# A four-layer graph kernel on one core: raw row-block loads issued as four transfers of 32 partitions from two queues

## The chip, the cores and the metric

The kernel runs on one core of a Trainium2 chip. The metric is the device time of one execution in microseconds (us), the median of the timed runs. All data are 32-bit floats.

## What is computed

Four graph layers act in turn on x (5120 nodes, 64 features) with one dense adjacency matrix adj (5120 x 5120, 105 MB). Each layer normalises x over its features, applies relu, multiplies by adj in its own way and adds the result to x:

```python
h = relu(layernorm(x)); x = x + L0(h, adj, ...)   # e = h + small product; adj @ (adj.T @ e), normalised, + h
h = relu(layernorm(x)); x = x + adj @ h           # L1
h = relu(layernorm(x)); x = x + L2(h, adj, ...)   # three products with adj, one after another
h = relu(layernorm(x)); x = x + L3(h, adj, ...)   # adj with unit diagonal, scaled by its row sums (degrees)
```

## The kernel before

The program has two stages. In the first, adj is read once from the chip's memory, is turned (transposed) on the way and is written back turned, as `adj_t`; at the same time the two products of the first layer and the row sums are made. In the second, five passes stream tiles of `adj_t` back in for the products that are left.

**Stage one.** adj is cut into 7 groups of columns (g), six of 768 columns and a last one of 512, and into 10 row blocks of 512 rows (m). A raw load brings one row block of one group, 128 partitions by 4 by 768 (1.5 MB), into `raw[:, m]`. Two row blocks make a pair, and five pairs make a group. A period of the steady state handles one pair, and the engines do this in it:

- TensorE turns the pair `after` into four PSUM banks that are used in rotation (`turn_banks`, L654), multiplies the pair before it, already turned, by t (`product_for_h`, L719 and L630), and multiplies two raw row blocks of the next group by E (`products_for_t`, L635 and L641). `products_for_t` waits for the raw load (L637).
- ScalarE copies each turned bank to `staged` (`copy_banks`, L853 and L869); TensorE needs the copy before it reuses the bank.
- VectorE turns the last chunk of each pair itself (`turn_chunk`, L1088 and L1105) and sums rows of raw (`sum_rows`, L1013 and L1016). Both wait for the raw load.
- The sync engine, SP, issues all large transfers in one order, written out by hand (L587 to L596): load of the first block of a pair for the next group, store of the turned pair (3 MB, L560), load of the second block. `load_next` (L567) waits until TensorE and VectorE have turned the pair (`wait_turned`) and until its rows are summed, since the load overwrites the same space.

Each raw load increments `raw_in[m]` by 16, and whoever reads waits for `g * 16 + 16`.

At the start SP issues the loads of x (three parts) and ten first loads (`load_first`, L545). ScalarE issues six small loads (L876 to L881), then copies `diag`, then squares and copies in turn for each row block (L882 to L890): these squares feed the first normalisation, and the chain ScalarE, VectorE, GpSimd, VectorE, TensorE is repeated per block until `e_ready` has reached 10. Then group 0 begins (L952).

**Stage two** begins near 523 us. Its tile loads (`load_turned`, L574) are issued by SP alone and span 128 partitions.

Of the kernel before, what the change touches and what calls it, by code (L numbers as in the profile page):

```python
# [10 lines left out]
P = 128  # L11
# [31 lines left out]
OPEN_BANKS = 5  # L43
EPS = 1e-5
SQ = 32
STAGE_WORDS = CHUNKS * PAIR
TILE_WORDS = 2 * PAIR

# [187 lines left out]
def gnn_stack(nc, x_d, adj_d, wu_d, du_d, pu_d, wi_d, di_d, pi_d, gam_d, bet_d, w2_d, b2_d, w3_d, b3_d, out_d):  # L236
    plan = Plan()
    ctx = ExitStack()
    with ctx:
# [188 lines left out]
        def raw_of(g, m):  # L428

            return raw_last[:, m] if g == NG - 1 else raw[:, m]  # L430
# [28 lines left out]
        def banks(g, m):  # L459

            return range(2 * chunks(g) - 2 * by_vector(g, m))
# [77 lines left out]
        @block.sync  # L539
        def _(sp):  # L540
            def load_x(i):
                t = slice(X_PARTS[i][0] * SUB, X_PARTS[i][1] * SUB)
                sp.dma_start(X[:, t, :], x_v[:, t, :]).then_inc(x_in[i], 16)

            def load_first(m):  # L545
                sp.dma_start(raw[:, m], adj_v[:, m, :, 0:GW]).then_inc(raw_in[m], 16)

            load_x(0)
            sp.dma_start(diag_rows[0:U // P, :], du_d.rearrange("(t p) -> t p", p=P)).then_inc(diag_in, 16)
            sp.dma_start(diag_rows[U // P:NT, :], di_d.rearrange("(t p) -> t p", p=P)).then_inc(diag_in, 16)  # L550
            load_x(1)
            load_first(0)
            load_x(2)
            for m in range(1, NB):
                load_first(m)

            def store(g, m):
                wait_copied(sp, g, m)
                at = g * CHUNKS * PAIR
                sp.dma_start(adj_t[m, :, at:at + STAGE_WORDS], staged_pair(g, m)).then_inc(stored_by(g, 2 * m)[0], 16)  # L560

            def store_kept(u):
                wait_copied(sp, NG - 1, u // 2, u % 2)
                at = (NG - 1) * CHUNKS * PAIR + u % 2 * TILE_WORDS
                sp.dma_start(adj_t[u // 2, :, at:at + TILE_WORDS], turned_into(NG - 1, u)).then_inc(stored_by(NG - 1, u)[0], 16)

            def load_next(g, m):  # L567

                wait_turned(sp, g, m // 2)
                sp.wait_ge(deg_summed, SUM_NO[g, m])  # L570
                src = adj_v[:, m, :, (g + 1) * GW:(g + 1) * GW + chunks(g + 1) * P]
                sp.dma_start(raw_of(g + 1, m), src).then_inc(raw_in[m], 16)

            def load_turned(n):  # L574

                p, m, k, dual = plan.tiles[n]
                j = plan.slot[n]
                sp.dma_start(whole[j], adj_t[m, :, k * TILE_WORDS:(k + 1) * TILE_WORDS]).then_inc(whole_in[j], 16)

            def first_load(n):  # L580
                p, m, k, dual = plan.tiles[n]
                g = (2 * k + 1) // CHUNKS
                for u in (2 * m, 2 * m + 1):
                    sp.wait_ge(*stored_by(g, u))
                load_turned(n)

            store(0, 0)  # L587
            load_next(0, 0)
            load_next(0, 1)
            for g in range(NG - 1):  # L590
                for i in range(ROWS):
                    after = (g, i + 1) if i + 1 < ROWS else (g + 1, 0)
                    if after[0] < NG - 1:
                        load_next(after[0], 2 * after[1])
                        store(*after)
                        load_next(after[0], 2 * after[1] + 1)  # L596
            first = iter(plan.loads[:len(AT_START)])
            first_load(next(first))
            sp.wait_ge(*stored_by(NG - 2, UNITS - 3))
            sp.wait_ge(used, unit_no(NG - 2, UNITS - 2))  # L600
            for _ in range(STAGE_WORDS // TILE_WORDS):
                first_load(next(first))
            store_kept(0)
            store_kept(1)
            sp.wait_ge(*stored_by(NG - 2, UNITS - 1))
            sp.wait_ge(used, unit_no(NG - 1, 0))
            for _ in range(LATE_SLOTS + 1 - STAGE_WORDS // TILE_WORDS):
                first_load(next(first))
            for u in range(2, UNITS):
                if u == UNITS - 1:  # L610
                    wait_turned(sp, NG - 1, u // 2)
                    sp.wait_ge(deg_summed, SUM_NO[NG - 1, u])
                    for n in first:
                        first_load(n)
                store_kept(u)
            for u in range(UNITS - 2, UNITS):
                sp.wait_ge(*stored_by(NG - 1, u))
            sp.wait_ge(used, TOTAL_UNITS)
            for n in plan.loads[len(AT_START):]:
                sp.wait_ge(multiplied, plan.used_no(plan.slot_before[n]))  # L620
                load_turned(n)
# [3 lines left out]
        def _(pe):  # L625
# [8 lines left out]

            def products_for_t(g, m):  # L635

                pe.wait_ge(raw_in[m], g * 16 + 16)  # L637
                columns = chunks(g) * P // 2
                for a in range(SUB):
                    for h in range(2):  # L640
                        last = nc.tensor.matmul(t_acc[h * D:(h + 1) * D, 0:columns], E[:, m * SUB + a, :],  # L641
                                                raw_of(g, m)[:, a, h * columns:(h + 1) * columns],
                                                start=(m == 0 and a == 0), stop=(m == NB - 1 and a == SUB - 1))
                if m == NB - 1:
                    last.then_inc(t_done, 1)
# [192 lines left out]
        def _(act):  # L838
# [33 lines left out]
            def copy_unit(g, u, some):  # L872

                copy_banks(g, u // 2, [u % 2 * chunks(g) + i for i in some if u % 2 * chunks(g) + i in banks(g, u // 2)])

            for i, src in ((0, pu_d), (2, pi_d)):  # L876
                act.dma_start(par[:, i:i + 2], src.partition_broadcast(P)).then_inc(early_in, 16)
            act.wait_ge(made, 2)
            for i, src in ((0, wu_d), (1, wi_d)):
                for h in range(2):  # L880
                    act.dma_start(w_in[h * D:(h + 1) * D, i, h * D:(h + 1) * D], src).then_inc(early_in, 16)  # L881
            act.wait_ge(diag_turned, 1)  # L882
            nc.scalar.activation(diag[:, :], t_rows[:, 0:NT], ACT.Copy).then_inc(diag_ready, 1)
            for m in range(NB + 2):
# [44 lines left out]
            def group(g):  # L929
                for i in range(ROWS):  # L930
                    after = (g, i + 1) if i + 1 < ROWS else (g + 1, 0)
                    begun = BEGUN if (g, i) == (0, 0) else 0
                    if i == 0:
                        copy_t(g)
                    copy_banks(*after, range(begun, TURN_BANKS))
                    if i == 0:
                        take_t(g)
                    copy_banks(*after, banks(*after)[TURN_BANKS:])

            def last_group():  # L940
                g = NG - 1
# [8 lines left out]
                    end_of_layer(u)  # L950

            act.wait_ge(e_ready, NB)  # L952
            for g in range(NG - 1):
                group(g)
            last_group()
# [37 lines left out]
        def _(dve):  # L993
# [18 lines left out]

            def sum_rows(g, m):  # L1013

                dve.wait_ge(raw_in[m], g * 16 + 16)
                nc.vector.tensor_reduce(deg_part[:, of(m), g], raw_of(g, m), AX.X, ALU.add).then_inc(deg_summed, 1)  # L1016


# [69 lines left out]
            def turn_chunk(g, m):  # L1088

                if by_vector(g, m):  # L1090
                    for b in range(2):
                        dve.wait_ge(raw_in[2 * m + b], g * 16 + 16)
                    if g < NG - 1:
                        wait_stage_free(dve, g, m)
                    elif m >= 1:
                        wait_turned(dve, g, m - 1)
                    else:
                        wait_turned(dve, g - 1, ROWS - 1)
                    half, c = chunks(g) // 2, chunks(g) - 1
                    rows = raw_flat if g < NG - 1 else raw_flat[:, 0:NB * SUB * CHUNKS_LAST * P]  # L1100
                    src = rows[:, :].rearrange("p (m a h k) -> p m h a k", m=ROWS, h=2, k=chunks(g) * P)[:, m]
                    dst = turned_into(g, 2 * m + 1)[:, (half - 1) * PAIR:half * PAIR].rearrange("p (h a n) -> p h a n", h=2, a=SUB)
                    for q in range(4):
                        for b in range(4):
                            last = nc.vector.transpose(dst[b * SQ:(b + 1) * SQ, :, :, q * SQ:(q + 1) * SQ],  # L1105
                                                       src[q * SQ:(q + 1) * SQ, :, :, c * P + b * SQ:c * P + (b + 1) * SQ])
                    last.then_inc(vector_turned, 1)
# [189 lines left out]
```

## Time and profile before

| what | value |
|---|---|
| timed runs | 1457.35 and 1459.07 us, median 1458.21 us |
| profiled execution, first to last instruction (span) | 1456.2 us |
| mean granted TensorE clock over the span | 0.997 |
| TensorE busy | 1422.6 us (98%) |
| moved by DMA | 523.23 MB, mean 359 GB/s |

The profiled execution's own time is its span and what lies around it. The page gives the span alone; the median of the timed runs is 2.0 us above it, and that is taken as what lies around. A busy share of TensorE counts modelled ends of pipelined matmuls, so a full share does not by itself say that TensorE is the bound: the timeline has to show that it never waits.

### The profile page before, as it was taken

To read this page: it belongs to the slowest core of one execution; us is meant where nothing else is said; L and a number is where in the kernel's file an instruction comes from. 1 tells how busy PE (TensorE), PEld (TensorE's weight loads), DVE (VectorE), ACT (ScalarE), POOL (GpSimd) and SP (SyncE) were. 2 spreads that over 40 slices of the span, in tenths; PEclk is the share of its full clock that TensorE was granted. 3 is DMA by queue.
4 is the path that set the end of the run, shared out by engine and by line. 5 is a ranking of instruction groups with operands and counts; after the bars stand their busy time and mean duration, and the time that the engine had idled before them with its cause. 6 is when DMAs were issued, how large, how long until landed. Compare 5 with 4: busy or idle time off the path is not lost.

```text
span 1456.2 us, 18041 instructions
## 1 busy us (share of the span) xinstructions
PE 1422.6 (98%) x7601; PEld 601.7 (41%) x7601; DVE 665.2 (46%) x1136; ACT 226.3 (16%) x453; POOL 84.3 (6%) x67
## 2 busy tenths in 40 slices
PE   6998999999999999999999999999999999999998
PEld 3553555555555554333333333333333333333332
DVE  6699999999998734320221311011311021101044
ACT  2331423333233342000000000000000000000000
POOL 2300000000000028100000000000000000000000
PEclk9999999999999999999999999999999999999999
DMA  9998999999999998999996897989797848996998
GB/s 325 386 379 354 406 415 418 411 419 413 412 416 368 381 418 324 421 421 420 420 420 211 323 354 298 359 323 315 300 348 263 302 179 362 392 380 228 354 415 321
DMA packets 97604, 523.23 MB, mean 359 GB/s; under 512 B 18764, under 2 KB 18804, under 8 KB 54644
## 3 DMA queue, kind: packets, MB, share of 16 engines
q1 hardware_dynamic: 90436, 520.40, 91.1%
q10 hardware_dynamic: 7088, 1.67, 0.5%
q8 instruction: 61, 1.00, 0.3%
q14 instruction: 19, 0.16, 0.0%
HBM read 415.88 MB, written 106.17 MB: 359 GB/s over the span
## 4 chain that ended last, share of the span: by engine, by line
PE 61%; DMA 2%; DVE 1%; POOL 0%; issue 0%; ACT 0%; DVEq 0%
PE turned L630 33%; PE acc L630 25%; DMA over_wide<-adj_t 2%; PE turned L663 1%; PE turned L815 1%; PE t_rows L799 0%; PE turned L821 0%; DVE staged L1143 0%; PE t_acc L789 0%; PE t_acc L715 0%; PE t_rows L715 0%; POOL rstd L1246 0%; DVE staged L1001 0%; DVE X L1189 0%; DVE staged L1205 0%
## 5 line engine op out<-in xcount | busy, mean ns | idle before, releaser
L1016 DVE TENSOR_REDUCE deg_part<-raw 128x4 f32<-128x3072 f32 (+1 forms) x70 | 220.8, 3196 | 0.9
L641 PE MATMUL t_acc<-raw,E 128*64 128x384 f32 (+1 forms) x1120 | 187.2, 483 | 10.8 <-DMA raw<-in_adj_dram 10.7
L1105 DVE STREAM_TRANSPOSE staged<-raw 32x256 f32<-32x256 f32 x448 | 195.1, 436 | 5.8
L869 ACT ACTIVATE staged<-turned 128x512 f32<-128x512 f32 x303 | 152.7, 640 | 240.8 <-PE turned L663 240.4
L630 PE MATMUL acc<-staged,t_cur 128*64 128x512 f32 x720 | 161.1, 597 | 0.0
L663 PEld LDWEIGHTS turned<-ident,raw 128*128 128x128 f32 x1376 | 150.1, 141 | 25.5 <-issue 25.5
L663 PE MATMUL turned<-ident,raw 128*128 128x128 f32 x1376 | 160.5, 275 | 0.0
L630 PE MATMUL turned<-over_last,C 128*64 128x512 f32 x672 | 152.1, 592 | 0.0
L641 PEld LDWEIGHTS t_acc<-raw,E 128*64 128x64 f32 x1120 | 79.4, 139 | 115.4 <-issue 89.2
L1246 POOL TENSOR_TENSOR rstd<-rstd,minus_half 128x8 f32<-128x8 f32 (+1 forms) x30 | 44.2, 1474 | 1279.6 <-DVE rstd L1007 1279.6
L630 PE MATMUL turned<-over_last,R 128*64 128x512 f32 x512 | 116.5, 593 | 0.0
L1217 DVE TENSOR_TENSOR staged<-turned,part 128x512 f32<-128x512 f32 x11 | 7.6, 692 | 225.8 <-PE turned L630 191.7
L630 PE MATMUL acc<-over_last,R 128*64 128x512 f32 x440 | 100.0, 593 | 0.0
L1143 DVE STREAM_TRANSPOSE staged<-staged 32x128 f32<-32x128 f32 x304 | 92.0, 303 | 4.5
L630 PEld LDWEIGHTS turned<-over_last,C 128*64 128x64 f32 x672 | 48.3, 137 | 95.4 <-issue 95.4
L630 PE MATMUL acc<-over_last,C 128*64 128x512 f32 x384 | 86.6, 593 | 0.0
L630 PEld LDWEIGHTS acc<-staged,t_cur 128*64 128x64 f32 x720 | 48.9, 137 | 90.8 <-issue 90.8
L1217 DVE TENSOR_TENSOR staged<-acc,part 128x512 f32<-128x512 f32 x8 | 5.5, 690 | 151.7 <-PE acc L630 83.5
L630 PE MATMUL turned<-over_last,E 128*64 128x512 f32 x320 | 74.1, 593 | 0.0
L630 PEld LDWEIGHTS turned<-over_last,R 128*64 128x64 f32 x512 | 36.2, 137 | 71.2 <-issue 69.3
L630 PE MATMUL acc<-staged,R 128*64 128x512 f32 x264 | 60.9, 595 | 0.5 <-DMA staged<-adj_t 0.5
L630 PEld LDWEIGHTS acc<-over_last,R 128*64 128x64 f32 x440 | 31.1, 137 | 61.6 <-issue 59.0
(137 smaller groups left out, 893.6 us busy)
## 6 DMA issues: line engine op xcount, KB each, us to landing
over_last<-adj_t SPq DMA_DIRECT2D x181, 1024.0 KB, 8.9
staged<-adj_t SPq DMA_DIRECT2D x91, 1024.0 KB, 9.7
raw<-in_adj_dram SPq DMA_DIRECT2D x60, 1536.0 KB, 18.4
adj_t<-staged SPq DMA_DIRECT2D x30, 3072.0 KB, 17.1
over_wide<-adj_t SPq DMA_DIRECT2D x23, 1024.0 KB, 7.1
raw<-in_adj_dram SPq DMA_DIRECT2D x10, 1024.0 KB, 15.0
adj_t<-over_last SPq DMA_DIRECT2D x8, 1024.0 KB, 12.2
adj_t<-C SPq DMA_DIRECT2D x2, 1024.0 KB, 21.7
```

What stands on the lines that cost most here:

```text
L630: last = nc.tensor.matmul(bank[h * D:(h + 1) * D, :], v[:, t + c, :], tile[:, (2 * c + h) * B:(2 * c + h + 1) * B], start=start and c == 0 ...
L641: last = nc.tensor.matmul(t_acc[h * D:(h + 1) * D, 0:columns], E[:, m * SUB + a, :], raw_of(g, m)[:, a, h * columns:(h + 1) * columns], st ...
L663: last = nc.tensor.transpose(turned[n % TURN_BANKS][:, a * P:(a + 1) * P], raw_of(g, 2 * m + b)[:, sub, c * P:(c + 1) * P], ident[:, :])
L815: last = nc.tensor.matmul(weigh_bank[odd][:, i * 4 * D:(i + 1) * 4 * D], feat_t[rows, nodes], w0123[rows, :, :].rearrange("p w d -> p (w d ...
L869: nc.scalar.activation(turned_into(g, u)[:, i * B:(i + 1) * B], turned[n % TURN_BANKS][:, :], ACT.Copy) \
L1016: nc.vector.tensor_reduce(deg_part[:, of(m), g], raw_of(g, m), AX.X, ALU.add).then_inc(deg_summed, 1)
L1105: last = nc.vector.transpose(dst[b * SQ:(b + 1) * SQ, :, :, q * SQ:(q + 1) * SQ], src[q * SQ:(q + 1) * SQ, :, :, c * P + b * SQ:c * P + (b ...
L1143: last = nc.vector.transpose(dst[b * SQ:(b + 1) * SQ, :, h, e, :], src[q * SQ:(q + 1) * SQ, :, b, :])
L1217: ins = nc.vector.tensor_tensor(y_sb[r % 2], bank, part[:, m, :], ALU.add)
L1246: op.tensor_tensor(v, v, minus_half[:, t(0)], ALU.pow).then_inc(pow_ready, 1)
```

## The change

Each raw load becomes four transfers of 32 partitions. SP issues those of partitions 0 to 63, ScalarE those of partitions 64 to 127. The semaphore then counts 64 for a load. ScalarE gets the ten first loads behind its six small ones, a `load_next` for blocks 0 and 1 behind its wait for `e_ready`, and one for each pair behind that pair's copies.

```diff
+QUARTERS = [slice(q * SQ, (q + 1) * SQ) for q in range(4)]
+SP_QUARTERS, ACT_QUARTERS = QUARTERS[:2], QUARTERS[2:]
+RAW_IN = 16 * len(QUARTERS)
 # SP
             def load_first(m):
-                sp.dma_start(raw[:, m], adj_v[:, m, :, 0:GW]).then_inc(raw_in[m], 16)
+                for q in SP_QUARTERS:
+                    sp.dma_start(raw[q, m], adj_v[q, m, :, 0:GW]).then_inc(raw_in[m], 16)
...
-                sp.dma_start(raw_of(g + 1, m), src).then_inc(raw_in[m], 16)
+                for q in SP_QUARTERS:
+                    sp.dma_start(raw_of(g + 1, m)[q], src[q]).then_inc(raw_in[m], 16)
 # TensorE, and the same in sum_rows and turn_chunk of VectorE
-                pe.wait_ge(raw_in[m], g * 16 + 16)
+                pe.wait_ge(raw_in[m], RAW_IN * (g + 1))
 # ScalarE
+            def load_first(m):
+                for q in ACT_QUARTERS:
+                    act.dma_start(raw[q, m], adj_v[q, m, :, 0:GW]).then_inc(raw_in[m], 16)
+            def load_next(g, m):
+                wait_turned(act, g, m // 2)
+                act.wait_ge(deg_summed, SUM_NO[g, m])
+                src = adj_v[:, m, :, (g + 1) * GW:(g + 1) * GW + chunks(g + 1) * P]
+                for q in ACT_QUARTERS:
+                    act.dma_start(raw_of(g + 1, m)[q], src[q]).then_inc(raw_in[m], 16)
...
+            for m in range(NB):
+                load_first(m)
             act.wait_ge(diag_turned, 1)
...
                     copy_banks(*after, banks(*after)[TURN_BANKS:])
+                    if after[0] < NG - 1:
+                        for m in range(2):
+                            load_next(after[0], 2 * after[1] + m)
...
             act.wait_ge(e_ready, NB)
+            for m in range(2):
+                load_next(0, m)
             for g in range(NG - 1):
```

ScalarE at the program's start, before (`par` and `w_in` are small weights, `staged<-h_acc` the squares of the first normalisation):

```order
L877 DMA par<-in_L_gnn_par_u_dram 128x2
L877 DMA par<-in_L_gnn_par_i_dram 128x2
L881 DMA w_in<-in_L_gnn_W_u_dram 64x64 [waits made]
L881 DMA w_in<-in_L_gnn_W_u_dram 64x64
L881 DMA w_in<-in_L_gnn_W_i_dram 64x64 x2
L883 ACT_TABLE_LOAD
L883 ACTIVATE diag<-t_rows 128x40 [waits diag_turned]
L845 ACTIVATE staged<-h_acc 128x256 [waits centred] x3
```

The same place of the changed program:

```order
L894 DMA par<-in_L_gnn_par_u_dram 128x2
L894 DMA par<-in_L_gnn_par_i_dram 128x2
L898 DMA w_in<-in_L_gnn_W_u_dram 64x64 [waits made]
L898 DMA w_in<-in_L_gnn_W_u_dram 64x64
L898 DMA w_in<-in_L_gnn_W_i_dram 64x64 x2
L883 DMA raw<-in_adj_dram 32x4x768 x20
L902 ACT_TABLE_LOAD
L902 ACTIVATE diag<-t_rows 128x40 [waits diag_turned]
L850 ACTIVATE staged<-h_acc 128x256 [waits centred] x3
```

Twenty transfers now stand ahead of ScalarE's first activation.

ScalarE from one pair of the steady state to the next, before (`staged<-turned` are the copies of a pair's ten turned banks; the waits on `used` and `stored` are for room in `staged`):

```order
L869 ACTIVATE staged<-turned 128x512 [waits used,stored0,chunk_turned]
L869 ACTIVATE staged<-turned 128x512 [waits chunk_turned] x9
L869 ACTIVATE staged<-turned 128x512 [waits used,stored1,chunk_turned]
L869 ACTIVATE staged<-turned 128x512 [waits chunk_turned] x9
L869 ACTIVATE staged<-turned 128x512 [waits used,stored0,chunk_turned]
```

The same place of the changed program:

```order
L874 ACTIVATE staged<-turned 128x512 [waits used,stored0,chunk_turned]
L874 ACTIVATE staged<-turned 128x512 [waits chunk_turned] x9
L891 DMA raw<-in_adj_dram 32x4x768 [waits deg_summed,vector_turned,chunk_turned]
L891 DMA raw<-in_adj_dram 32x4x768
L891 DMA raw<-in_adj_dram 32x4x768 [waits deg_summed,vector_turned,chunk_turned]
L891 DMA raw<-in_adj_dram 32x4x768
L874 ACTIVATE staged<-turned 128x512 [waits used,stored1,chunk_turned]
L874 ACTIVATE staged<-turned 128x512 [waits chunk_turned] x9
```

Between the copies of one pair and those of the next ScalarE now waits for VectorE's part of the pair (`vector_turned`) and issues four transfers. On SP the order of loads and stores stays, with two transfers of 32 partitions in place of each raw load.

## Rows read from the trace of the kernel before

**Rows 1.** The page, its head and its first part: busy time by engine.

```profile
span 1456.2 us, 18041 instructions
...
PE 1422.6 (98%) x7601; PEld 601.7 (41%) x7601; DVE 665.2 (46%) x1136; ACT 226.3 (16%) x453; POOL 84.3 (6%) x67
```

**Rows 2.** Stretches: length, busy by engine, then granted clock, DMA share, GB/s.

```profile
45.00:60.00 15.00, 15.00 (x96) 7.39 (x92) 7.60 (x7) 1.75 (x4) 4.63 (x1) 1.00 1.02 409
...
135.00:150.00 15.00, 10.49 (x60) 6.72 (x60) 14.77 (x20) 4.64 (x10) 0.00 (x0) 0.77 1.02 419
...
435.00:450.00 15.00, 14.84 (x95) 7.83 (x94) 13.85 (x19) 5.13 (x12) 0.00 (x0) 1.00 1.02 417
...
800.00:1000.00 200.00, 199.87 (x938) 67.17 (x936) 34.71 (x96) 5.75 (x11) 1.64 (x1) 1.00 0.87 330
```

**Rows 3.** Timeline of TensorE in steady periods: start, length, what, [idle before].

```profile
250.66 4.58 PE L663 MATMUL turned<-ident,raw 128*128 128x128 f32 x40
...
265.64 4.59 PE L663 MATMUL turned<-ident,raw 128*128 128x128 f32 x40
...
433.75 4.59 PE L663 MATMUL turned<-ident,raw 128*128 128x128 f32 x40
...
446.38 2.80 PE L641 MATMUL t_acc<-raw,E 128*64 128x384 f32 x16 [0.17 <-DMA raw<-in_adj_dram]
449.12 1.97 PE L663 MATMUL turned<-ident,raw 128*128 128x128 f32 x16
```

**Rows 4.** DMA issues: count, KB each, median us from issue to landing.

```profile
raw<-in_adj_dram SPq DMA_DIRECT2D x60, 1536.0 KB, 18.4
adj_t<-staged SPq DMA_DIRECT2D x30, 3072.0 KB, 17.1
```

**Rows 5.** Who waited for whom, whole span: total us, times, longest.

```profile
PEld t_acc L641 <- DMA raw<-in_adj_dram: 20.7, 17, 6.2
```

**Rows 6.** Issues by line: duration min/median/max in ns, first and last start.

```profile
L546 SPq DMA_DIRECT2D raw<-in_adj_dram x10: 532/3754/6989, 2.8 to 31.0; - x10
...
L987 ACTq DMA_DIRECT2D out_dram<-staged x5: 378/378/410, 1409.5 to 1453.2; - x5
```

**Rows 7.** Timeline of ScalarE at the start and at its late small loads.

```profile
3.24 1.27 ACTq L881 DMA_DIRECT2D w_in<-in_L_gnn_W_i_dram  x2
...
6.57 0.20 ACT L883 ACTIVATE diag<-t_rows 128x40 f32<-128x40 f32 x1 [0.74 <-PE t_rows L673]
...
55.17 0.45 ACTq L896 DMA_DIRECT2D b<-in_L_gnn_b_dram  x1
```

**Rows 8.** Timeline: VectorE in the first chain, SP's first next load, its first reader.

```profile
9.30 0.42 DVE L1011 SCALAR_TENSOR_TENSOR h_acc<-h_acc,rstd 128x256 f32<-128x256 f32 x1
...
11.50 0.16 DVE L1032 TENSOR_TENSOR par<-par 128x1 f32<-128x1 f32 x1 [1.78 <-DMA w_in<-in_L_gnn_W_i_dram]
...
40.61 4.31 SPq L572 DMA_DIRECT2D raw<-in_adj_dram  x2
...
70.06 5.33 PE L641 MATMUL t_acc<-raw,E 128*64 128x384 f32 x32
```

**Rows 9.** DMA queues (q10 is ScalarE's): packets, MB, share of 16 engines.

```profile
q10 hardware_dynamic: 7088, 1.67, 0.5%
```

**Rows 10.** Timelines of VectorE and ScalarE: the late VectorE, and a steady period.

```profile
105.97 5.01 ACT L869 ACTIVATE staged<-turned 128x512 f32<-128x512 f32 x10 [9.97 <-PE turned L663]
122.15 5.00 ACT L869 ACTIVATE staged<-turned 128x512 f32<-128x512 f32 x10 [11.18 <-PE turned L663]
...
112.58 7.17 DVE L1105 STREAM_TRANSPOSE staged<-raw 32x256 f32<-32x256 f32 x16
...
428.93 7.18 DVE L1105 STREAM_TRANSPOSE staged<-raw 32x256 f32<-32x256 f32 x16
...
434.44 5.00 ACT L869 ACTIVATE staged<-turned 128x512 f32<-128x512 f32 x10 [10.36 <-PE turned L663]
449.23 0.49 ACT L903 ACTIVATE t_t<-t_acc 128x384 f32<-128x384 f32 x1 [9.78 <-PE t_acc L641]
```

More of the change, by code:

```diff
@@ L1013, in sum_rows @@
             def sum_rows(g, m):
-                dve.wait_ge(raw_in[m], g * 16 + 16)
+                dve.wait_ge(raw_in[m], RAW_IN * (g + 1))
                 nc.vector.tensor_reduce(deg_part[:, of(m), g], raw_of(g, m), AX.X, ALU.add).then_inc(deg_summed, 1)
@@ L1091, in turn_chunk @@
                     for b in range(2):
-                        dve.wait_ge(raw_in[2 * m + b], g * 16 + 16)
+                        dve.wait_ge(raw_in[2 * m + b], RAW_IN * (g + 1))
                     if g < NG - 1:
```

## The prediction, on record before the changed kernel ran

> **What bounds the kernel now.** I read the page's head first, then the stretches, then TensorE's timeline, then who waits for the raw loads. The head shows a span of 1456.2 us with TensorE busy 98% of it [rows 1]; the reader is to see that TensorE is nearly always at work, and to ask whether anything else is as full. The stretches answer that: between 435 and 450 us TensorE is busy 14.84 of 15 us and the DMA engines have a share of 1.02 at 417 GB/s, so both are full at once; between 800 and 1000 us, in stage two, TensorE is busy 199.87 of 200 us at a DMA share of 0.87 [rows 2]. Stage two is TensorE's alone, and the change does not touch it. The question is stage one.
>
> There the timeline gives the two paces. A period is from the first turn of a pair to that of the next. From 250.66 to 265.64 it is 14.98 us and TensorE's rows show no wait. From 433.75 to 449.12 it is 15.37 us, and the second block of the pair is waited for, by 0.17 us beyond the last matmul [rows 3]. So late in the stage the transfers set the pace. The bytes agree: two loads of 1536 KB and a store of 3072 KB [rows 4] are 6.29 MB, and at 417 GB/s that is 15.1 us. In all, raw loads are waited for 20.7 us [rows 5]. That is the most that a better delivery of loads could give back; whatever slows the loads is paid almost one for one, since no slack is left in 14.98 against 15.1 us.
>
> **The start of ScalarE.** Twenty transfers come ahead of its first activation. Its six small loads end at 3.24 + 1.27 = 4.51 us, each of the last two having taken 0.64 us [rows 7]; its cheapest issue of the trace took 378 ns [rows 6]. At a middle 0.5 us, twenty take 10 us, and ScalarE is free at 14.5 us; before, it ran its first activation at 6.57 us, when its input was there [rows 7]. The chain behind it: VectorE's first normalised block came at 9.30 us, 2.73 us later, and ran 0.42 us; the step behind that then waited for a small load until 11.50 us [rows 8]. Now the block ends at 14.5 + 2.73 + 0.42 = 17.65 us, 17.65 - 11.50 = 6.2 us later than the step could go on. Nothing catches that up: TensorE is busy 15.00 of 15 us between 45 and 60 us [rows 2]. I take **+6.2 us**. Below: at 378 ns an issue ScalarE is free at 12.1 us, and +3.7 us is left. Above: SP's ten first issues took 3754 ns in the median and up to 6989 [rows 6], so an issue can be held until earlier ones drain; the last began at 31.0 us. Were ScalarE held until 31 us, the cost would be +22.7 us. I stay near the lower end, since ScalarE's queue has half the bytes of SP's queue of before.
>
> **The steady state on ScalarE.** Each pair adds four issues behind its copies. In the late period the copies run from 434.44 to 439.44 us and the next activation comes 9.78 us after that; four issues at 0.45 us (the last of the small late loads [rows 7]) are 1.8 us and lie in that gap. The new wait for VectorE ends before it begins: VectorE's part ran from 428.93 to 436.11 us [rows 10]. The exception is where VectorE is late: its part ran from 112.58 to 119.75 us, ScalarE's copies ended at 110.98, and the next were due at 122.15 [rows 10]. ScalarE stands there until 119.75, issues until 121.6, and the copies queued behind it are still in time, with 0.5 us to spare. If the cover fails there, TensorE, which needs the copies for its banks, pays 2 us once or twice. The first next loads move more: before at 40.61 us, now behind the late small loads, which end at 55.62 us [rows 7]; their reader starts at 70.06 us [rows 8]. That leaves 14.4 us against a median landing of 18.4 for a whole load [rows 4]. ScalarE's queue is then empty and holds half a load, so I take 0, with 4 us as the other end.
>
> **More transfers.** 70 raw loads become 280 transfers, 210 more. Each ends in small packets. ScalarE's queue of before moved only small ones: 7088 packets in 0.5% of 16 engines' span [rows 9], which is 0.005 x 1456.2 x 16 / 7088 = 16 ns each. One per engine and transfer gives 210 x 16 ns = **+3.4 us**; below, 0, as the packets may fall into idle time.
>
> **The pace of a 32-partition load.** This is the term that decides, and the trace cannot show it: every large transfer of before spans 128 partitions. The descriptors stay as they were (one row of 768 floats), so the lower bound is the present pace, 417 GB/s, and +0. The upper bound: a transfer that reaches a quarter of the partitions at a time goes at half pace. Then the 3.15 MB of loads of a period take 15.1 instead of 7.55 us, +7.5 us a period. From 145 us, where VectorE is no longer late, to the stage's end near 523 us there are (523 - 145) / 15.2 = 25 periods with DMA as full as this. So the bound is 25 x 7.5 = +188 us. Below zero: -20.7 us, all waits for raw loads gone [rows 5]; more is excluded, since TensorE's own 14.98 us remain.
>
> Between them I reason from the order. ScalarE's queue loads partitions 64 to 127, SP's 0 to 63. While both are loading, the whole width is written and the pace should hold. But SP also has the store, 3.15 MB, ahead of its second load; ScalarE has 1.57 MB in all per period, SP 4.72. If the queues share evenly, ScalarE's part runs out beside the store, and SP's 1.57 MB of loads then goes alone, on half of the partitions. All of it alone at half pace is +3.8 us a period, none is 0. I take half, +1.9 us, nearer to the row of today's pace than to the upper end: 25 x 1.9 = **+47.5 us**.
>
> The Trainium skill, SBUF — State Buffer, "Door 1: The DMA port swizzle (why `[64,N]` ≈ `[32,N]`)", speaks against the change: partitions 0 to 31 reach 8 of 16 ports, partitions 0 to 63 the same 8, and 189 GB/s were measured for 32 partitions against 328 for 128. No run here shows it. Its section "Can I just issue two DMAs to hit both halves?" adds that two concurrent transfers at partitions 0 and 64 gained only 6% over one; by that, loads stay near half pace and the sum is that of the second rival below.
>
> **The sum.** The profiled execution's span is 1456.2 us; 2.0 us more give the median of the timed runs, 1458.2. With +6.2, +3.4 and +47.5 it comes to **1515 us**.
>
> **The rivals.**
> 1. *The loads keep their pace.* The halves of the two queues overlap, and only the start and the packets cost: 1458.2 + 6.2 + 3.4 = 1468 us. For it: descriptors and bytes are the same, and the DMA share of 1.02 [rows 2] says that it is the engines that are full, whose work is unchanged. Against it: SP's queue has three times the bytes of ScalarE's. It decides if ScalarE's loads last as long as SP's loads do.
> 2. *Half pace throughout.* 1468 + 188 = 1656 us. For it: the order puts the two quarters of one queue one behind the other. Against it: two queues on opposite halves run at once. Here TensorE would wait several us in each period, and its clock may go: after the wait between 135 and 150 us, where it was busy 10.49 of 15 us, the granted clock averaged 0.77 in that stretch [rows 2], against 1.00, so some of it was granted at the lower level, 1.2 GHz.
> 3. *Faster: loads arrive earlier.* ScalarE's half of the second block is not behind the store. If that ends the waits for raw loads and the start is hidden, 1458.2 - 20.7 = 1437 us. Against it: SP's half still stands behind the store, and a load counts when its last quarter has landed. It begins to decide only if the queues together move more than 417 GB/s.
>
> That the change does not do what it says is no rival: the order shows the transfers on both engines.
>
> **How the numbers follow.** Forecast 0.44, rival one 0.40, rival two 0.12, rival three 0.04. A measurement of this kernel can tell about 2% from no change, 29 us: faster is below 1429, slower above 1487. Rival three reaches faster with its tail, 0.03. Same takes rival one but for a costly start (0.36), the rest of rival three (0.01) and the lower tail of the forecast (0.05): 0.42. Slower is what is left, 0.55. The range holds the time 8 times in 10: from 1461, just under rival one with the cheapest start (1465), to 1640, which leaves out most of rival two. The forecast's own range is 1490 to 1570. Most of the chance lies on the side of a cost; a gain over 2% has hardly any.
>
> **What would show it.** Right: ScalarE's first activation near 14.5 us; steady periods near 17 us in place of 15.37, with waits for raw loads on TensorE in each; GB/s below 417 in stage one at a DMA share that stays near 1; stage two as long as before. Wrong: periods still at 15.4 us (rival one), near 22 us (rival two), or 14.98 without waits (rival three); or a ScalarE that is held beyond 20 us at the start, which would make the start the largest term.

## The result, and the profile after

The changed kernel takes 1520.01 us (median; the runs are 1517.52 and 1522.5) against 1458.21: a ratio of 1.0423, 95% interval 1.0406 to 1.0440. It is slower by 62 us. The prediction said 1515. The sum was right, but three of its terms were not: the start was put far too low, the pace and the packets too high, and the errors nearly cancelled.

The page of the changed kernel: head, busy time, the two hardware queues (packets, MB, share of 16 engines), and the issues (count, KB each, median us to landing).

```profile
span 1515.3 us, 18310 instructions
...
PE 1426.8 (94%) x7601; PEld 602.7 (40%) x7601; DVE 665.0 (44%) x1136; ACT 226.3 (15%) x453; POOL 84.3 (6%) x67
...
q1 hardware_dynamic: 73636, 467.98, 80.7%
q10 hardware_dynamic: 27248, 54.11, 11.8%
...
raw<-in_adj_dram SPq DMA_DIRECT2D x120, 384.0 KB, 20.0
raw<-in_adj_dram ACTq DMA_DIRECT2D x120, 384.0 KB, 15.9
```

TensorE does the same work as in [rows 1], 1426.8 against 1422.6 us, in a span that is 59.1 us longer: nearly all of the lost time is idle time of TensorE. A quarter of a load (384 KB) takes 20.0 us (SP) and 15.9 us (ScalarE) to land, about as long as a whole load of 1536 KB did [rows 4].

Where it was lost is read from a landmark that occurs once per group. TensorE's `t_rows` product comes seven times, once per group; shown are the first, second, sixth and last of these marks, first before, then after.

```profile
60.94 0.49 PE L706 MATMUL t_rows<-ident,t_t 128*128 128x128 f32 x3
146.96 0.49 PE L706 MATMUL t_rows<-ident,t_t 128*128 128x128 f32 x3
...
450.92 0.49 PE L706 MATMUL t_rows<-ident,t_t 128*128 128x128 f32 x3
520.71 0.38 PE L706 MATMUL t_rows<-ident,t_t 128*128 128x128 f32 x2
```

```profile
89.64 0.55 PE L711 MATMUL t_rows<-ident,t_t 128*128 128x128 f32 x3 [1.56 <-ACT t_t L922]
178.61 0.49 PE L711 MATMUL t_rows<-ident,t_t 128*128 128x128 f32 x3
...
511.64 0.49 PE L711 MATMUL t_rows<-ident,t_t 128*128 128x128 f32 x3
580.36 0.38 PE L711 MATMUL t_rows<-ident,t_t 128*128 128x128 f32 x2
```

The difference of the pairs is 28.7, 31.7, 60.7 and 59.7 us. So 28.7 us are lost before the first mark, some 31 more through stage one, and nothing after it (span: +59.1). Of these 31, 3.0 come up to the second mark and 29.1 in the 20 periods from the second to the sixth, which take 333.0 us in place of 304.0; 1.1 are won back behind it.

**The start.** ScalarE's timeline after, and one row of VectorE's.

```profile
4.55 30.09 ACTq L883 DMA_DIRECT2D raw<-in_adj_dram  x20
...
35.97 0.20 ACT L902 ACTIVATE diag<-t_rows 128x40 f32<-128x40 f32 x1
```

```profile
38.81 0.16 DVE L1056 TENSOR_TENSOR par<-par 128x1 f32<-128x1 f32 x1
```

The twenty issues end at 34.64 us, not at 14.5. ScalarE's first activation comes at 35.97 in place of 6.57, and the step of VectorE that had gone on at 11.50 [rows 8] goes on at 38.81, 27.3 us later. Here is the spread of these issues (ns, minimum, median, maximum):

```profile
L883 ACTq DMA_DIRECT2D raw<-in_adj_dram x20: 453/644/8273, 4.6 to 26.4; - x20
```

A median of 644 ns is close to what was assumed; but single issues stand for up to 8.3 us. The engine's own work waits behind them.

The queues in the first 40 us, after and then before (the last row in each is the third part of x, us to landing):

```profile
q10 hardware_dynamic: 2506, 5.27, 63.5%
q1 hardware_dynamic: 5653, 2.57, 36.0%
...
X<-in_x_dram SPq DMA_DIRECT2D x1, 640.0 KB, 41.9
```

```profile
q1 hardware_dynamic: 9201, 13.17, 94.2%
...
X<-in_x_dram SPq DMA_DIRECT2D x1, 640.0 KB, 11.2
```

In that time ScalarE's queue (q10) brought 5.27 MB and SP's 2.57: for most of it mainly partitions 64 to 127 were being loaded, and x's third part took 30.7 us longer to land.

**The pace.** Stretches after, columns as in [rows 2], then one of before.

```profile
20.00:25.00 5.00, 0.00 (x0) 0.00 (x0) 0.00 (x0) 0.00 (x0) 0.00 (x0) 1.00 1.07 217
...
45.00:50.00 5.00, 5.00 (x22) 2.12 (x22) 3.60 (x8) 0.42 (x1) 1.11 (x1) 1.00 1.03 336
50.00:55.00 5.00, 4.67 (x34) 3.01 (x33) 4.87 (x9) 1.05 (x3) 1.11 (x1) 1.00 1.04 321
...
60.00:65.00 5.00, 5.00 (x37) 3.21 (x37) 4.90 (x8) 1.34 (x3) 0.83 (x1) 1.00 1.04 201
...
300.00:400.00 100.00, 92.54 (x587) 49.88 (x585) 86.02 (x115) 31.16 (x63) 0.00 (x0) 1.00 1.02 382
...
800.00:1000.00 200.00, 199.88 (x944) 67.74 (x942) 43.51 (x121) 8.52 (x17) 3.27 (x2) 1.00 0.83 323
```

```profile
300.00:400.00 100.00, 99.52 (x624) 52.53 (x622) 92.46 (x121) 32.58 (x66) 0.00 (x0) 1.00 1.02 414
```

The reader is to see a DMA share of 1 or more in every stretch of stage one, at rates that differ by a factor of two: 217 GB/s while ScalarE's queue loads its half and SP's is busy with x, 321 to 336 while both load, 201 when x has landed and SP's half alone is left, 382 in the steady state with the store among them, 414 before. A full share says that the engines are occupied, not that they move what they can. Stage two (800 to 1000) is as before.

A steady period on TensorE after, and its waits for raw loads over the whole span (us, times, longest):

```profile
308.36 2.80 PE L646 MATMUL t_acc<-raw,E 128*64 128x384 f32 x16 [1.34 <-DMA raw<-in_adj_dram]
311.09 4.59 PE L668 MATMUL turned<-ident,raw 128*128 128x128 f32 x40
...
324.90 2.80 PE L646 MATMUL t_acc<-raw,E 128*64 128x384 f32 x16 [1.34 <-DMA raw<-in_adj_dram]
327.63 2.62 PE L668 MATMUL turned<-ident,raw 128*128 128x128 f32 x22
```

```profile
PEld t_acc L646 <- DMA raw<-in_adj_dram: 56.1, 29, 3.6
```

This period is 327.63 - 311.09 = 16.54 us, 1.17 more than the late 15.37 of [rows 3] and 1.56 more than the earlier 14.98; the second block of each pair is waited for by 1.34 us, where it was 0.17 or nothing. The mean of the 20 periods between the marks is 29.1 / 20 = 1.45 us more than before.

Within a period the loss can be placed. The two queues between 303 and 306 us, while both load and no packet of the store is among them (packets, MB, share):

```profile
q10 hardware_dynamic: 163, 0.45, 52.3%
q1 hardware_dynamic: 164, 0.45, 51.5%
```

They move 300 GB/s together. Between 309 and 315 us, with the store among them, it is 411 to 427; before, no 1.5 us between 433 and 448 us had less than 356. ScalarE's queue does not run dry in this period: in each stretch of 3 us from 300 to 333 its share is 9.7% or more.

### The profile page after: what moved, and what is told of

The parts are those of the page before. It is cut to its first block, busy times and chain, and to the rows that moved or that the text cites. A ratio compares the mean times of both kernels' runs of the same rounds, so it can differ in the third digit from the quotient of the medians.

```text
span 1515.3 us, 18310 instructions
## 1 busy us (share of the span) xinstructions
PE 1426.8 (94%) x7601; PEld 602.7 (40%) x7601; DVE 665.0 (44%) x1136; ACT 226.3 (15%) x453; POOL 84.3 (6%) x67
## 2 busy tenths in 40 slices
DMA packets 100966, 523.26 MB, mean 345 GB/s; under 512 B 22124, under 2 KB 22164, under 8 KB 58004
## 4 chain that ended last, share of the span: by engine, by line
PE 58%; DMA 2%; DVE 1%; POOL 0%; issue 0%; ACT 0%; DVEq 0%
PE turned L635 31%; PE acc L635 24%; DMA over_wide<-adj_t 2%; PE turned L668 1%; PE turned L820 1%; PE t_rows L804 0%; PE turned L826 0%; DVE staged L1167 0%; PE t_acc L794 0%; PE t_acc L720 0%; PE t_rows L720 0%; POOL rstd L1270 0%; DVE staged L1227 0%; DVE staged L1241 0%; DVE staged L1035 0%
## 5 line engine op out<-in xcount | busy, mean ns | idle before, releaser
L646 PE MATMUL t_acc<-raw,E 128*64 128x384 f32 (+1 forms) x1120 | 191.0, 486 | 37.3 <-DMA raw<-in_adj_dram 37.3
## 6 DMA issues: line engine op xcount, KB each, us to landing
raw<-in_adj_dram ACTq DMA_DIRECT2D x120, 384.0 KB, 15.9
```

## The experiments

Unless said otherwise, each edit is made on the changed kernel, and costs in us are (ratio - 1) x 1458.2. Where the number of transfers of a load changes, the counts that readers wait for change with it; these lines are left out of the cuts.

**One part alone (two kernels).** The first loads whole again, by SP; only the next ones split:

```diff
 # load_first
-for q in SP_QUARTERS: sp.dma_start(raw[q, m], adj_v[q, m, :, 0:GW]) ...
+sp.dma_start(raw[:, m], adj_v[:, m, :, 0:GW]) ...
-ScalarE: for m in range(NB): load_first(m)
```

> The changed kernel, but the ten first loads are again one transfer of 128 partitions each, by SP; the later loads stay in quarters on two queues. Theory A (the start costs 27 us because ScalarE's issues are held until 34.67 us, the rest of the 62 us is a slower period): about 1520 - 27 = 1493 us, ScalarE's first activation at 6.6 us, steady periods still 16.5 us. Rival B (the whole loss is the pace of narrow loads in the steady state, the late start is hidden): 1515 to 1520 us.

Measured: 1489.0 us, ratio 1.0210 [1.0193, 1.0227], +30.6 us. ScalarE's first activation is at 6.75 us, and the waits in the periods stay (1.32 and 0.96 us at 311.50 and 327.99).

The reverse: only the first loads split, the next ones whole and by SP.

```diff
 # load_next
-for q in SP_QUARTERS: sp.dma_start(raw_of(g + 1, m)[q], src[q]) ...
+sp.dma_start(raw_of(g + 1, m), src) ...
-ScalarE: load_next(...)
```

> The kernel of before, but with the ten first loads in quarters on two queues as in the changed kernel; all later loads are one transfer by SP. Theory A: 1458 + 27 = 1485 us, first activation of ScalarE near 34.7 us, steady periods 15.0 to 15.4 us as before. Rival B: 1458 to 1465 us.

Measured: 1487.29 us, 1.0199 [1.0183, 1.0214], +29.0 us. ScalarE is held as in the changed kernel (its twenty issues take 30.71 us); the stretch from 300 to 400 us is back at before's rate:

```profile
300.00:400.00 100.00, 99.34 (x625) 52.62 (x623) 92.86 (x126) 30.91 (x62) 0.00 (x0) 1.00 1.02 416
```

30.6 + 29.0 = 59.6 us of 61.7: two separate costs that add up, each about half.

**Four transfers of 128 partitions.** As many transfers, the same two queues, the same rows of 768 floats; but each transfer takes one of the four rows of a partition, over all partitions.

```diff
-QUARTERS = [slice(q * SQ, (q + 1) * SQ) for q in range(4)]
+QUARTERS = [slice(q, q + 1) for q in range(4)]
-raw[q, m], adj_v[q, m, :, 0:GW]
+raw[:, m, q], adj_v[:, m, q, 0:GW]
```

> The changed kernel with the same four transfers per load, two by SP and two by ScalarE, but each takes all 128 partitions and one of the four rows of a partition, in place of 32 partitions and all four rows. Theory A (the pace is lost because a quarter, and one queue's two quarters, reach only half of the partitions): steady periods back at 15.0 to 15.4 us, DMA near 417 GB/s; the first loads drain at twice the pace, so ScalarE is free near 17 us in place of 34.67 and the start costs about 10 us: 1468 to 1472 us. Rival C (the cost is that there are four transfers and two queues): 1515 to 1520 us, periods 16.5 us.

Measured: 1479.84 us, 1.0147 [1.0132, 1.0162], +21.4 us: far from the rival's time, but above the theory's 1468 to 1472.

```profile
4.59 18.05 ACTq L883 DMA_DIRECT2D raw<-in_adj_dram  x20
```

```profile
15.00:20.00 5.00, 0.00 (x0) 0.00 (x0) 0.00 (x0) 0.00 (x0) 0.00 (x0) 1.00 1.06 375
```

At 375 GB/s in place of 217, ScalarE is still held until 22.64 us. So the hold is not made by the half width, only lengthened by it. Its first `t_rows` comes at 76.39 us, 15.5 late, and stage one ends 542.01 - 520.71 = 21.3 late: the pace costs 6 us in place of 31.

**The same width, first loads whole.**

```diff
 # on the kernel above: load_first as in the first experiment
```

> First loads whole by SP as in the kernel before; later loads as four transfers of all 128 partitions and one row each, two by SP and two by ScalarE. Theory A (the pace depends on the width alone): 1456 to 1462 us, periods 15.0 to 15.4 us. Rival G (two queues cost something of their own: the wide rows run had periods of 15.8 to 16.3 us late in the stage): 1463 to 1470 us.

Measured: 1462.48 us, 1.0032 [1.0021, 1.0042], +4.7 us. Against the first experiment (+30.6) only the shape of the next loads differs.

**The same width, all by SP.**

```diff
 # on the kernel of four wide transfers
-for q in SP_QUARTERS: sp.dma_start(...)
+for q in QUARTERS: sp.dma_start(...)
-ScalarE: load_first, load_next
```

> Every raw load as four transfers of all 128 partitions and one row each, all issued by SP, none by ScalarE. Theory A (width sets the pace; the small loss of the two-queue wide run, 1462.5 us, is the two queues' own): 1456 to 1460 us. Rival H (that small loss is the number of transfers): 1461 to 1465 us.

Measured: 1453.83 us, 0.9973 [0.9963, 0.9983], 3.9 us faster than before. The same 280 transfers cost nothing in sum. The two kernels differ by 8.6 us (4.7 + 3.9), but not in the second queue alone: one has its first loads whole, the other in four wide transfers. The first `t_rows` of the kernel on two queues, then that of this one:

```profile
60.85 0.55 PE L710 MATMUL t_rows<-ident,t_t 128*128 128x128 f32 x3 [0.38 <-ACT t_t L919]
```

```profile
58.48 0.49 PE L711 MATMUL t_rows<-ident,t_t 128*128 128x128 f32 x3
```

So 2.4 us lie before the first mark; 525.22 - 516.89 = 8.3 us lie between the two at the last. What is left for the second queue at full width is some 6 us.

**The quarters of 32 partitions, all by SP.**

```diff
-for q in SP_QUARTERS: sp.dma_start(raw[q, m], ...)
+for q in QUARTERS: sp.dma_start(raw[q, m], ...)
-ScalarE: load_first, load_next
```

> Quarters of 32 partitions as in the changed kernel, but all four issued by SP, one behind the other, none by ScalarE. Theory A (a quarter alone goes at half pace; only the other queue's quarters on the other half of the partitions bring some of it back): steady periods near 15.4 + 7.5 = 22.9 us, stage one about 190 us longer, 1640 to 1680 us; the first loads at about 210 GB/s. Rival D (what costs is the issue on ScalarE): 1460 to 1470 us.

Measured: 1626.48 us, 1.1150 [1.1074, 1.1227], +168 us, somewhat under the theory's 1640 to 1680. TensorE's timeline with its first `t_rows`, and the stretch:

```profile
92.04 0.49 PE L711 MATMUL t_rows<-ident,t_t 128*128 128x128 f32 x3
...
333.17 4.59 PE L668 MATMUL turned<-ident,raw 128*128 128x128 f32 x40
...
350.85 5.33 PE L646 MATMUL t_acc<-raw,E 128*64 128x384 f32 x16 [5.21 <-DMA raw<-in_adj_dram]
356.11 4.59 PE L668 MATMUL turned<-ident,raw 128*128 128x128 f32 x40
...
373.66 1.53 PE L668 MATMUL turned<-ident,raw 128*128 128x128 f32 x12
```

```profile
300.00:400.00 100.00, 79.92 (x457) 41.09 (x454) 71.07 (x95) 23.03 (x47) 0.00 (x0) 0.90 1.01 306
```

Here are periods of 22.9 us, the half pace of the prediction's second rival, but also of 17.6 us. The mean of the 20 between the second and the sixth mark (200.59 and 601.00 us) is 20.0, so the second rival's size is not reached; why the periods differ was not taken apart. What the changed kernel has over this one is ScalarE's queue on the other half. The granted clock from 300 to 400 us is 0.90, so part of it ran at 1.2 GHz; this follows the waits of up to 5.2 us. The first mark is 31.1 us late although ScalarE issues no raw load and runs its first activation at 6.78 us: here TensorE waits for the first raw blocks, by up to 4.98 us at a time. So first loads at half pace are costly at the start even where nothing holds ScalarE.

**Both queues on the same half at once.** SP takes quarters 0 and 2, ScalarE 1 and 3.

```diff
-SP_QUARTERS, ACT_QUARTERS = QUARTERS[:2], QUARTERS[2:]
+SP_QUARTERS, ACT_QUARTERS = QUARTERS[0::2], QUARTERS[1::2]
```

> The changed kernel, but SP takes partitions 0 to 31 and 64 to 95 of each load and ScalarE 32 to 63 and 96 to 127, so that the two queues work on the same half of the partitions at the same time. Theory A (the halves 0 to 63 and 64 to 127 each go at half pace, and only opposite halves together bring some of it back): nearly nothing is brought back, periods of 19 to 22 us, about as the kernel with all quarters on SP (1626 us) or somewhat slower, since the start is late as well: 1620 to 1660 us. Rival E (any two quarters from two queues go at the same pace, whichever they are): 1515 to 1525 us.

Measured: 1574.51 us, 1.0800 [1.0778, 1.0822], +117 us. Its second and sixth `t_rows`:

```profile
180.96 0.49 PE L711 MATMUL t_rows<-ident,t_t 128*128 128x128 f32 x3
...
562.84 0.49 PE L711 MATMUL t_rows<-ident,t_t 128*128 128x128 f32 x3
```

The 20 periods take 381.9 us, 19.1 each. Single ones reach 329.73 - 308.98 = 20.8 us, with waits of 4.4 and 4.0 us. The first mark is that of the changed kernel (89.77 and 89.64 us), so the difference lies in the pace. The bytes, transfers and queues are those of the changed kernel; which partitions the queues reach at the same time makes 55 us. The time lies between the two that were expected. That the queues do not stay in step would make the loss smaller than the theory's; this is not shown.

**Halves of 64 partitions.** One transfer for each queue, the same two halves.

```diff
-QUARTERS = [slice(q * SQ, (q + 1) * SQ) for q in range(4)]
-SP_QUARTERS, ACT_QUARTERS = QUARTERS[:2], QUARTERS[2:]
+QUARTERS = [slice(q * 2 * SQ, (q + 1) * 2 * SQ) for q in range(2)]
+SP_QUARTERS, ACT_QUARTERS = QUARTERS[:1], QUARTERS[1:]
```

> The changed kernel with two transfers per load, SP partitions 0 to 63 and ScalarE 64 to 127, in place of four: half the number of transfers, the same halves and queues. Theory A (what counts is the half that a queue reaches, not the number of transfers): 1512 to 1522 us, periods 16.5 us, ScalarE held to about 30 us at the start. Rival C (the number of transfers costs): half of the loss is gone, about 1490 us.

Measured: 1522.38 us, 1.0439 [1.0423, 1.0454]: the changed kernel's time with half its transfers. Its first `t_rows`:

```profile
90.71 0.49 PE L711 MATMUL t_rows<-ident,t_t 128*128 128x128 f32 x3
```

ScalarE's ten issues of 768 KB end at 29.39 us, 5.3 us earlier than the changed kernel's twenty, and yet the first mark is 1.1 us later. So the hold alone does not set the mark; x's third part took 43.3 us to land here.

**Fewer first loads on ScalarE.** Only the first five blocks are split at the start; SP loads the other five whole.

```diff
 # load_first, SP
+if m < 5: quarters as now
+else: sp.dma_start(raw[:, m], ...)
-ScalarE: for m in range(NB): load_first(m)
+ScalarE: for m in range(5): load_first(m)
```

> The changed kernel, but only the first five row blocks come in quarters at the start, ten transfers by ScalarE in place of twenty; the other five come whole from SP. Theory A (ScalarE is held because its queue is full: 34.67 us was reached when about 86 of its 160 row packets per engine had gone, so some 75 fit): ten transfers are 80 packets and nearly fit, ScalarE is free at 10 to 13 us, and the start costs 2 to 10 us in place of 28: 1495 to 1503 us. Rival F (each issue on ScalarE takes 1.5 us beside a busy SP): free at 4.6 + 15 = 20 us, the start costs 14 us, about 1506 us.

Measured: 1512.53 us, 1.0370 [1.0339, 1.0402]. ScalarE's ten issues end at 10.27 us, as the theory had it; but little was won, since something else was late next:

```profile
38.02 0.69 PE L690 MATMUL t_rows<-ident,staged 128*128 128x128 f32 x2 [12.04 <-DVE staged L1064]
...
80.90 0.55 PE L714 MATMUL t_rows<-ident,t_t 128*128 128x128 f32 x3 [2.67 <-ACT t_t L925]
```

VectorE had waited for the third part of x, which took 31.4 us to land. It stands behind the first raw load in SP's queue. The first mark is still 20.0 us late, and the time is above both that were expected.

**The same, with x's third part ahead of the first raw load on SP.**

```diff
 load_x(1)
+load_x(2)
 load_first(0)
-load_x(2)
```

> As the run with ten first transfers on ScalarE (1512.5 us), and SP issues the third part of x ahead of its first raw load. Theory A (there TensorE stood 12 us at 38 us because the third part of x, 160 small packets per engine, went one for one with ScalarE's slow row packets and landed at 35.8 us): the part lands before 12 us, that wait is gone and the start costs 2 to 8 us: 1492 to 1498 us. Rival I (what is late at the start is the raw blocks, since they come at half pace): 1508 to 1513 us.

Measured: 1509.08 us, 1.0336 [1.0305, 1.0368]: the theory missed, and the time is the rival's. x lands in 15.0 us, the wait of 12 us is gone, and the first `t_rows` comes at 69.41:

```profile
69.41 0.55 PE L714 MATMUL t_rows<-ident,t_t 128*128 128x128 f32 x3 [1.19 <-ACT t_t L925]
```

So up to this mark the start now costs 8.5 us. But TensorE waits for the first next loads instead, 6.12 us at 84.87 and 5.49 at 95.36, and of the 20.2 us won against the changed kernel at the first mark 8.9 are left at the last. So not all of what the start costs can be had by mending it alone; how the rest is lost was not taken apart further.

**The store behind both loads.** An edit on the kernel before: SP's order for a pair becomes load, load, store.

```diff
 load_next(after[0], 2 * after[1])
-store(*after)
 load_next(after[0], 2 * after[1] + 1)
+store(*after)
```

> The kernel of before with one change in SP's order: both whole loads of a pair are issued ahead of the store, in place of load, store, load. If the waits for raw loads that are left (20.7 us) come from the second load standing behind the 3 MB store, most of them go and the time is 1440 to 1450 us. If the DMA engines' own work per period sets the pace (15.1 to 15.3 us against 14.98 us of TensorE), the store comes late in place of the load: 1453 to 1460 us.

Measured: 1450.21 us, 0.9947 [0.9935, 0.9960]: 7.7 us faster than before, and so faster than both kernels. Its `t_rows`, and its waits (us, times, longest) on transfers:

```profile
136.15 0.49 PE L706 MATMUL t_rows<-ident,t_t 128*128 128x128 f32 x3
...
510.10 0.38 PE L706 MATMUL t_rows<-ident,t_t 128*128 128x128 f32 x2
```

```profile
ACT staged L869 <- DMA adj_t<-staged: 53.7, 8, 10.2
```

It is 10.8 us ahead of before at the second mark, 6.6 at the third (215.58 against 222.18 us) and 10.6 at the last; its span is 8.2 us shorter. So the early waits, which are also where before's clock fell to 0.77 [rows 2], are the largest part of the gain; some of it is given back at once, and the last group wins again. TensorE's waits for raw loads are gone from the view. In their place ScalarE now waits for room in `staged`; where TensorE feels that, it is 2.27 us at 138.91.

**Both gains together.** The store last, on the four wide transfers by SP.

```diff
 # the kernel with all wide transfers on SP
 load_next(after[0], 2 * after[1])
-store(*after)
 load_next(after[0], 2 * after[1] + 1)
+store(*after)
```

> The four transfers of 128 partitions by SP alone, with the store behind both loads of a pair. Theory (their two gains have different places, the first chain at the start and the waits for raw loads in the steady state, and add up): 1458.2 - 4.4 - 8.0 = 1445.8 us, 1444 to 1448. Rival one (both take away the same waits for raw loads): 1450, as the store's move alone. Rival two (loads split in four let the store's packets in sooner, and copies then wait for room in staged): 1454 or more.

Measured: 1451.95 us, 0.9960 [0.9946, 0.9973]. The interval overlaps that of the store's move alone: the gains do not add. The time lies between those of the two rivals, so it does not decide between them.

```profile
ACT staged L874 <- DMA adj_t<-staged: 167.3, 21, 11.0
```

ScalarE waits three times as long for the stores as above.

## Why the prediction was right in its sum and wrong in three terms

**What bounds the kernel: right.** Stage one had no slack. What the loads lost was paid almost one for one, stage two did not move, and of the 20.7 us of waits [rows 5] the two kernels that show none won 7.7 and 5.8.

**The start of ScalarE: the hold named, the size wrong and other causes missed.** The term was +6.2 us; the runs show 28.7 at the first mark, and 29.0 for that part alone. The step that failed is "I stay near the lower end, since ScalarE's queue has half the bytes of SP's queue of before". The prediction's upper bound, ScalarE held until 31 us, was read from SP's row [rows 6], and it is what happened (34.6 us). Ten issues of 384 KB go in without that (free at 10.27 us); twenty do not, even at full width (22.64 us), and neither do ten of 768 KB (29.39 us), so it is not the number of issues that counts. On SP, which computes nothing, such a stall holds up only further transfers; on ScalarE the first chain stands behind it. And the queue was not emptied at 417 GB/s: mainly one half was being loaded, and 217 GB/s were moved. The prediction's list of what would show it wrong had this case: "a ScalarE that is held beyond 20 us at the start".

The hold is not all, though. With ScalarE free at 10.27 us, 20.0 of the 28.7 us are left, and x's third part is late; with x in front as well 8.5 are left; and with all quarters on SP, where ScalarE is not held and x takes 14.4 us, TensorE waits for the first raw blocks, and the mark is 31.1 us late. The term had only the first of these. How the 28.7 us divide among them can't be said, since they overlap.

**The steady state on ScalarE: right, 0.** The four issues of a pair lie in the gap before the next copies, which still wait for TensorE:

```profile
311.79 4.51 ACT L874 ACTIVATE staged<-turned 128x512 f32<-128x512 f32 x9 [11.54 <-PE turned L668]
```

**The first next loads: 0 is borne out where the start is that of before.** In the changed kernel 3.0 us are lost between the first two marks. In the kernel with whole first loads this stretch takes 148.26 - 61.53 = 86.7 us against 86.0, so less than 1 us is lost there, the pace's loss included. The early waits of before lie in the same stretch and may hide some of it.

**More transfers: wrong, 0 in place of +3.4 us.** The count was right: the page of after has 100966 packets, that of before 97604, which is 16 for each of the 210 added transfers. The cost does not show: half as many transfers of the same halves take the same time, and 280 wide ones by SP, with as many packets, beat the 70 of before.

**The pace: the right cause, the wrong place and too large.** It is the width that costs: the next loads in quarters cost 30.6 us, in wide rows on the same queues 4.7. The term was 25 periods at +1.9 us, 47.5 in all; measured are 20 periods at 1.45, 29.1 us, 31 by the first and last marks and 30.6 by the kernel that has this part alone. Both factors were too high. The five periods of the last group load only 512 columns and lost nothing (68.7 us between the last two marks, 69.8 before). And "I take half" stood on the step that failed: "While both are loading, the whole width is written and the pace should hold", so that only SP's loads, going alone, would lose. The rows show the low rate where both load, 300 GB/s between 303 and 306 us, and ScalarE's queue did not run out. The second rival's half pace of 22.9 us a period is real in single periods, but needs one queue (+168 us in all); two queues on the same half cost 117.

On the width the Trainium skill, SBUF — State Buffer, "Door 1: The DMA port swizzle (why `[64,N]` ≈ `[32,N]`)", says that 64 partitions in a row reach no more ports than 32; the trace agrees, with 201 to 217 GB/s on one half alone against 417 [rows 2] and the same time for transfers of 64 as of 32. Its section "Can I just issue two DMAs to hit both halves?" has only 6% more for two; here both halves together moved 321 to 336 GB/s against 217, 48% to 55% more, so the measurement decides. The prediction's sentence that by this section the sum is that of the second rival did not come out: 1520 us against 1656.

The errors, +22.5 at the start against -16.5 and -3.4 in the pace and the packets, nearly cancel. That the sum came out within 5 us is luck and no evidence for its terms; the two kernels with one part each are what shows them.

## What to carry to other kernels

Split a load over its rows, not over its partitions, if it has to be split: four wide transfers from one queue cost nothing here, and quarters of 32 partitions cost 62 us from two queues and 168 from one, the start included. Before large transfers are given to an engine that also computes, find out how much its queue takes and what stands behind the issue, at the program's start above all. And where a load and a store compete on one queue, look at their order first: moving the store behind the loads won 7.7 us, with no transfer changed.

## What the runs showed of the hardware that was not expected

- The issuing engine stood within single issues for up to 8.3 us, while their median was 644 ns; a median of issues says nothing of this.
- x's third part (640 KB) took 41.9 us to land in place of 11.2 when ScalarE's queue loaded beside it. With all quarters on SP's queue it took 14.4. The two queues' shares in the first 40 us, 63.5% and 36.0%, fill the same 16 engines.
- A DMA share of 1 or more went with 201, 217, 300, 336, 382 and 414 GB/s, in stretches that differ in which partitions were being reached.
- Open are: why both halves together stay at 300 to 336 GB/s and do not reach 417; why a second queue costs some 6 us at full width; why the periods of one queue's quarters differ by 5 us; and where the gain goes that the reordered x gives at the start. These were not tried further.
